# Expert results of an octet gathered in one transfer with 4 KB pieces, the last two octets from two queues, and stages separated by one meeting instead of two

## The reference

```python
x = x + tanh(g_xattn[0]) * L0_xattn(ctx, layernorm(x), mask, ...)   # 2 heads of 64, rms-normed q and k
x = x + tanh(g_ffn[0])   * L0_ffn(layernorm(x), ...)                # soft experts: 16 x 64 slots, hidden 256
x = x + tanh(g_xattn[1]) * L1_xattn(ctx, layernorm(x), ...)         # 8 heads of 128
x = x + tanh(g_ffn[1])   * L1_ffn(layernorm(x), ...)                # 8 experts, the best 2 of each token
```

```python
xf = x.reshape(N, D)                                   # N = 4096 tokens, D = 128
routing = softmax(xf @ router_w.T)                     # 8 experts
top_w, top_i = top_k(routing, 2); top_w = top_w / sum(top_w)
g = einsum('nd,ehd->neh', xf, w_gate); u = einsum('nd,ehd->neh', xf, w_up)
y = einsum('neh,edh->ned', silu(g) * u, w_down)        # hidden 256
out = einsum('ned,ne->nd', y, combine)                 # combine: top_w at the two experts, else 0
```

## Time and profile before

| what | us |
|---|---|
| three runs, median (lowest to highest) | 1481.29 (1478.18 to 1482.33) |
| span of the profiled execution | 1498.2 |
| PE busy in it | 1377.6 (92%) |
| ACT busy | 1012.3 (68%) |
| DVE busy | 953.4 (64%) |
| POOL busy | 523.2 (35%) |

### The profile page before, as it was taken

The page is one execution under the profiler, slowest core; times in us unless marked ns, Lnnn a source line. Parts: engine busy times, 40 slices in busy tenths (PEclk is TensorE's granted clock), DMA queues, the critical chain, the costliest instruction groups (busy, mean ns, idle before and its releaser), DMA issues. The chain is left out here.

```text
span 1498.2 us, 33716 instructions
## 1 busy us (share of the span) xinstructions
PE 1377.6 (92%) x12029; PEld 1171.5 (78%) x12029; DVE 953.4 (64%) x2374; ACT 1012.3 (68%) x2019; POOL 523.2 (35%) x510
## 2 busy tenths in 40 slices
PE   5898699899999999999999999988999999876985
PEld 4887588788888888888888888877778888755773
DVE  6998767666766767667667666552455555654455
ACT  5887487577677676776776767647788888633552
POOL 3112355322322322323223223302235555635553
PEclk9999899999999999999999999999999999998998
DMA  8300100399940000000000000022000000022236
GB/s 221 88 1 1 58 2 1 77 176 102 102 30 2 2 1 2 2 2 2 2 2 1 2 1 2 1 73 57 1 29 14 17 16 16 30 69 63 76 97 174
DMA packets 124980, 60.46 MB, mean 40 GB/s; under 512 B 41945, under 2 KB 120241, under 8 KB 124690
## 3 DMA queue, kind: packets, MB, share of 16 engines
q1 hardware_dynamic: 120274, 48.92, 18.2%
q0 software_dynamic: 4544, 9.38, 1.9%
HBM read 28.84 MB, written 29.44 MB: 39 GB/s over the span
## 5 line engine op out<-in xcount | busy, mean ns | idle before, releaser
L1349 DVE SCALAR_TENSOR_TENSOR hidden<-psU,b_cols,gelu 128x512 f32<-128x512 f32 x256 | 191.4, 750 | 170.1 <-ACT gelu L1474 104.9
L1474 ACT ACTIVATE gelu<-psG,b_cols 128x512 f32<-128x512 f32 x256 | 176.2, 689 | 109.6 <-PE psG L142 96.2
L1296 POOL TENSOR_TENSOR combine_sum<-combine_sum,combineT 128x512 f32<-128x512 f32 x48 | 63.3, 1319 | 294.9 <-ACT combineT L1488 294.9
L1325 POOL TENSOR_TENSOR dispatchT<-dispatchT,dispatch_inv 128x512 f32<-128x512 f32 x64 | 67.7, 1057 | 232.6 <-DVE dispatch_inv L1453 232.6
L1608 PE MATMUL psU<-w_down,hidden 128*64 128x128 f32 x2048 | 123.4, 273 | 0.0
L1608 PE MATMUL psDown<-w_down,hidden 128*64 128x128 f32 x2048 | 122.7, 273 | 0.0
L1861 POOL TENSOR_TENSOR probs<-probs,row_sum 128x512 f32<-128x512 f32 x64 | 66.2, 1035 | 143.6 <-DVE row_sum L1974 142.6
L1608 PEld LDWEIGHTS psU<-w_down,hidden 128*64 128x64 f32 x2048 | 113.2, 137 | 1.3 <-issue 1.2
L1608 PEld LDWEIGHTS psDown<-w_down,hidden 128*64 128x64 f32 x2048 | 113.9, 137 | 0.1
L140 PE MATMUL psG<-slots_hi,w_gate_hi 128*128 128x512 f32 x256 | 105.9, 414 | 1.1 <-ACT gelu L1474 0.6
L2038 ACT ACTIVATE probs<-psS,neg_max 128x128 f32<-128x128 f32 x256 | 91.2, 384 | 22.8 <-DVE neg_max L1971 18.4
(11 more groups left out here) (406 smaller groups left out, 3617.6 us busy)
## 6 DMA issues: line engine op xcount, KB each, us to landing
sorted_x<-empty_rows SPq DMA_DIRECT2D x1, 12736.0 KB, 77.5
tile_rows<-sorted_x SPq DMA_DIRECT2D x78, 65.0 KB
sorted_x<-empty_rows SPq DMA_DIRECT2D x1, 4544.0 KB, 29.9
expert_ys<-expert_y SPq DMA_DIRECT2D x16, 256.0 KB, 3.7
x<-in_x SPq DMA_DIRECT2D x8, 256.0 KB, 5.9
ctx<-in_ctx SPq DMA_DIRECT2D x8, 256.0 KB, 5.9
w_gate_raw<-in_L_ffn_Wg SPq DMA_DIRECT2D x1, 2048.0 KB, 10.9
w_up_raw<-in_L_ffn_Wu SPq DMA_DIRECT2D x1, 2048.0 KB, 16.1
```

What stands on the lines that cost most here:

```text
L1325: pool.tensor_tensor(e[:], e[:], over(rb[:], SEQ, 2), ALU.mult).then_inc(s["eb_normed"], 1)
L1349: dve.scalar_tensor_tensor(hid[e][:, half, :], U[half][:], bcol[:, 1, 4 * ch + 2 * e + half:][:, 0:1], gel[half][:], ALU.add, ALU.mult).th ...
L1474: act.activation(gel[half][:], G[half][:], ACT.Gelu, bias=bcol[:, 0, 4 * ch + 2 * e + half:][:, 0:1]).then_inc(s["gelu"], 1)
```

## The change

Four things are changed.

1. Home is now 8 p + 2 (t in the octet) + k, plus 1024 for each octet before it in the group. The eight results that partition p needs for one octet (four pairs, two choices) are eight rows in a row, 4096 bytes. `constants_vector` builds it with the same doubling steps; one instruction replaces the last two.
2. An octet is gathered in one transfer of 512 KB, 4096 bytes a partition, into `yin` with the choice behind the pair. Octets 0 to 6 are gathered by SP, octet 7 (`LAST`) by ACT, which waits for the same landed scatters at the end of its stream.
3. Of octet 7, DVE adds only the first two pairs (two adds of 128x256) and POOL the other two (two adds of 128x256, counted by the new semaphore `added_pool`); SP waits for both before its store.
4. `clear` no longer makes the engines meet, except after `stage_attention0` (`reused=True`). In exchange the semaphores of the stage just ended are kept out of the next one's choice.

```diff
-    def sem(self, ctx):
+    def sem(self, ctx, reused=False):
-        sems = []
+        sems, cleared = [], self.cleared
         def clear():
             self.nc.clear_and_free_semaphores(sems)
-            self.nc.all_engine_barrier()
+            if reused:
+                self.nc.all_engine_barrier()
+            self.cleared = [] if reused else [sem.num for sem in sems]
         def make(name):
-            sems.append(self.nc.alloc_semaphore(name=name))
+            num = [n for n in self.nc.free_semaphores if n not in cleared][0]
+            sems.append(self.nc.alloc_semaphore(name=name, num=num))
...
-        dve.tensor_copy(self.home[:, 0, 0:1], self.index[:]).then_inc(s["home"], 1)
-        for n, m in enumerate((1, 2, 4, 8, 16)):
+        dve.tensor_scalar(self.home[:, 0, 0:1], self.index[:], float(2 * OP), None, ALU.mult).then_inc(s["home"], 1)
+        for n, (m, step) in enumerate(((1, 2), (2, 4), (4, 2 * OT), (8, 4 * OT), (16, 8 * OT))):
...
-        for g, r in ((0, slice(0, first)), (1, slice(first, PAIRS))):
-            dve.tensor_scalar(self.home[:, 1, r], self.home[:, 0, r], float(self.groups[g].tokens), None, ALU.add
-                              ).then_inc(s["home"], 1)
+        dve.tensor_scalar(self.home[:, 1, :], self.home[:, 0, :], 1.0, None, ALU.add).then_inc(s["home"], 1)
...
+        def gather(eng, o):
+            group = R.groups[R.group_of(o)]
+            at = (o - group.octets[0]) * 2 * OT
+            eng.dma_start(yin[:, o, :, :, :].rearrange("p t k d -> p (t k d)"),
+                          group.ys[at:at + 2 * OT, :].rearrange("(p r) d -> p (r d)", p=P)).then_inc(y_loaded[o], 16)
...
-            for o in GROUPS[1]:
-                gather(o)
-            for o in GROUPS[1]:
-                store(o)
+            wait_stored(sp, len(QUADS) - 1)
+            gather(sp, LAST - 1)
+            store(LAST - 1)
+            sp.wait_ge(s["added"], 2 * OCTETS)
+            sp.wait_ge(s["added_pool"], 2)
+            sp.dma_start(tokens(c.out)[:, OP * LAST:OP * LAST + OP, :], c.x[:, OP * LAST:OP * LAST + OP, :]).then_inc(c.stored, 16)
...
+            pool.wait_ge(y_loaded[LAST], 16)
+            for k in range(2):
+                need(pool, s["added_pool"], k)
+                xo = c.x[:, OP * LAST + 2:OP * LAST + OP, :]
+                pool.tensor_tensor(xo, xo, yin[:, LAST, 2:OP, k, :], ALU.add).then_inc(s["added_pool"], 1)
...
-                xo = c.x[:, OP * o:OP * o + OP, :]
-                dve.tensor_tensor(xo, xo, yin[:, o, k, :, :], ALU.add).then_inc(s["added"], 1)
+                n = OP if o < LAST else 2
+                xo = c.x[:, OP * o:OP * o + n, :]
+                dve.tensor_tensor(xo, xo, yin[:, o, 0:n, k, :], ALU.add).then_inc(s["added"], 1)
...
+            wait_stored(act, len(QUADS) - 1)
+            gather(act, LAST)
```

More of the change, by code:

```diff
@@ L105, in __init__ @@
         self.stored = keep.enter_context(nc.semaphore("out_stored"))
+        self.cleared = []
     def sb(self, ctx):
@@ L239, in constants_vector @@
         first = self.groups[0].span
-        dve.tensor_copy(self.home[:, 0, 0:1], self.index[:]).then_inc(s["home"], 1)
-        for n, m in enumerate((1, 2, 4, 8, 16)):
+        dve.tensor_scalar(self.home[:, 0, 0:1], self.index[:], float(2 * OP), None, ALU.mult).then_inc(s["home"], 1)
+        for n, (m, step) in enumerate(((1, 2), (2, 4), (4, 2 * OT), (8, 4 * OT), (16, 8 * OT))):
             dve.wait_ge(s["home"], n + 1)
             w = min(m, first - m)
-            dve.tensor_scalar(self.home[:, 0, m:m + w], self.home[:, 0, 0:w], float(m * P), None, ALU.add
+            dve.tensor_scalar(self.home[:, 0, m:m + w], self.home[:, 0, 0:w], float(step), None, ALU.add
                               ).then_inc(s["home"], 1)
@@ L612, in stage_attention0 @@
     with ExitStack() as ctx:
-        sb, sem = c.sb(ctx), c.sem(ctx)
+        sb, sem = c.sb(ctx), c.sem(ctx, reused=True)
         ready = Ready(c, lined_up(nc))
@@ L2249, in stage_experts1 @@
         to = [sb(f"tile_to{i}", [P, OP], U32) for i in range(SPARE)]
-        yin = sb("expert_ys", [P, OCTETS, 2, OP, D])
+        yin = sb("expert_ys", [P, OCTETS, OP, 2, D])
         XT, ROUTE = c.bank(ctx, "psXT"), c.bank(ctx, "psRoute")
@@ L2255, in stage_experts1 @@
         Y = [c.bank(ctx, f"psY3_{i}") for i in range(2)]
-        names = "xt x_hi x_lo gu silu hidden ht ht_copied down scaled to_ready added"
+        names = "xt x_hi x_lo gu silu hidden ht ht_copied down scaled to_ready added added_pool"
         s = {n: sem("d_" + n) for n in names.split()}
@@ L2262, in stage_experts1, with wait_stored @@
         block = ctx.enter_context(nc.Block())
+        def gather(eng, o):
[3 more added lines that the diff above has]
+                          group.ys[at:at + 2 * OT, :].rearrange("(p r) d -> p (r d)", p=P)).then_inc(y_loaded[o], 16)
+        def wait_stored(eng, q):
+            for last in range(q + 1 - SPARE, q + 1):
+                eng.wait_ge(stored[last % SPARE], 16 * upto(last, SPARE))
         @block.sync
@@ L2269, in load @@
                 R.load_tiles(sp, q)
-            def gather(o):
-                group = R.groups[R.group_of(o)]
-                at = (o - group.octets[0]) * OT
-                for k in range(2):
-                    sp.dma_start(yin[:, o, k, :, :], group.ys[k * group.tokens + at:k * group.tokens + at + OT, :]
-                                 .rearrange("(t p) d -> p t d", p=P)).then_inc(y_loaded[o], 16)
             def store(o):
-                need(sp, s["added"], 2 * (o + 1))
+                sp.wait_ge(s["added"], 2 * (o + 1))
                 sp.dma_start(tokens(c.out)[:, OP * o:OP * o + OP, :], c.x[:, OP * o:OP * o + OP, :]).then_inc(c.stored, 16)
@@ L2285, in _ @@
                 load(q)
-            for last in range(QUAD[NA - 1] + 1 - SPARE, QUAD[NA - 1] + 1):
-                sp.wait_ge(stored[last % SPARE], 16 * upto(last, SPARE))
+            wait_stored(sp, QUAD[NA - 1])
             for o in GROUPS[0]:
-                gather(o)
+                gather(sp, o)
             for o in GROUPS[0]:
                 store(o)
-            for last in range(len(QUADS) - SPARE, len(QUADS)):
-                sp.wait_ge(stored[last % SPARE], 16 * upto(last, SPARE))
-            for o in GROUPS[1]:
-                gather(o)
-            for o in GROUPS[1]:
-                store(o)
+            wait_stored(sp, len(QUADS) - 1)
[4 more added lines that the diff above has]
+            sp.dma_start(tokens(c.out)[:, OP * LAST:OP * LAST + OP, :], c.x[:, OP * LAST:OP * LAST + OP, :]).then_inc(c.stored, 16)
             sp.wait_ge(c.stored, 16 * OCTETS)
@@ L2349, in add @@
             def add(o, k):
-                dve.wait_ge(y_loaded[o], 32)
+                dve.wait_ge(y_loaded[o], 16)
                 need(dve, s["added"], 2 * o + k)
-                xo = c.x[:, OP * o:OP * o + OP, :]
-                dve.tensor_tensor(xo, xo, yin[:, o, k, :, :], ALU.add).then_inc(s["added"], 1)
+                n = OP if o < LAST else 2
+                xo = c.x[:, OP * o:OP * o + n, :]
+                dve.tensor_tensor(xo, xo, yin[:, o, 0:n, k, :], ALU.add).then_inc(s["added"], 1)
             x_lo(0)
```

## The result

The changed kernel takes 1484.70 us (median of 9 executions, 1482.79 to 1487.88), the kernel before 1481.35 us (9 executions, 1478.18 to 1482.33). The ratio is 1.0029, with a 95% interval of 1.0019 to 1.0039, which is 4.3 us (2.8 to 5.8). The forecast was 1479.6 us, a range of 1476.2 to 1482.0 and a chance of 0.10 for slower.

The account below looks back on a forecast made before the run. PE was busy 92%, but gains were sought where every engine waits: the stage borders and the end's chain of waits. Terms -0.7 - 0.7 - 0.5 + 0.2 = -1.7 us took 1481.29 to 1479.6 us, range 1476.2 to 1482.0.

Parts of the forecast that it names:

- added waits: At the end, SP's wait for POOL's adds has only the last store behind it; no cost was counted.
- dear scatters: Rival: the new row spacing makes POOL's last-stage scatters take 1.85 us each, 9 us more, 1488.6 us; chance 0.08.
- closing drains: At the end, POOL's two drains of 0.10 us and its clears remain, so dropping two meetings wins 0.5 us.
- Second meetings: Four meetings go: 0.7 us won at each of two inner borders and 0.5 us at the end.
- Gathers: Octets 6 and 7 land together at 1490.9, after 1.4 us fixed and 2.6 us of transfer at 406 GB/s.
- Larger pieces: Rival: 4096-byte pieces in the last gathers still move at 280 GB/s, sum -0.5 us, 1480.8 us; chance 0.18.
- The fixed part: Start cost of a last gather, taken as 1.4 us from the last store's 2.3 us wait.
- Adds in turns: DVE's and POOL's last adds wait for each other, taking 3.6 us and ending at 1494.5, a term of +0.2 us.
- Ending 7.4 to 7.8 us after SP's first gather: Sign that the forecast is right: the last adds end then, against 7.35 us before.
- octet 6's store: Near the end, this store was expected to have gone out 1 us sooner than before.
- Hidden edits: Gathers of octets 0 to 5, constants and row spacing count 0; bounds for the last scatter's landing -0.2 to +1.8 us.

Follow-up runs that it names:

- share_only: The kernel before with only POOL's two adds of octet 7 added: 1483.82 us against 1479.24 us, ratio 1.0035.
- no_share: The changed kernel with all last adds on DVE and none on POOL: 1477.85 us against 1479.24 us for the kernel before, ratio 0.9995.
- early_drain: The changed kernel with one more drain of POOL ahead of its two adds: 1478.59 us against 1479.24 us for the kernel before, ratio 1.0001.
- meetings_only: The kernel before without the second meetings except after the first stage: 1478.37 us against 1479.24 us, ratio 0.9991.
- one_queue: The changed kernel with all adds on DVE and both last gathers issued by SP: 1477.06 us against 1478.31 us for the kernel before, ratio 0.9988.
- the second comparison: The changed kernel measured again, unchanged, against the kernel before: 1484.07 us against 1478.42 us, ratio 1.0033.

## Why the prediction was wrong, point by point

**The step that failed** is in the part on added waits: "SP waits for POOL's adds with only the last store behind". It looked at what stands behind the waiting SP and not at what stands behind POOL's adds. There stood the block's closing drain, a row of the very line that I quoted for SP's branch, and it was 8.95 us long. Moved behind the adds, it ended at 1485.19 where SP was ready at 1480.8. This is worth 4.6 us by SP's wait and 5.3 us in the end of share_only (4.6 by its medians), and it disappears in no_share and early_drain. None of the rivals had it; the one that ended slower, dear scatters, was tested and is not so.

I had also counted the closing drains as two of 0.10 us, from the line that clears semaphores. That was right for those two. The Trainium skill (VectorE: DVE Perf Modes, The DRAIN you can't avoid) gives "~12 ns constant" for the drains that the runtime puts at the start and end of a kernel on all five engines. These here carry the line of the program's own block, SP's is 7 ns and POOL's 8849 ns long, so that figure is not to be carried over to them.

**Second meetings, a second step that failed.** "At the two inner borders each engine starts 0.7 us sooner" held, but the sum took it for 1.4 us of the total. The third stage took 321.1 to 321.3 us from release to release in seven of eight profiles without the second meeting, against 320.6 to 320.8 in three of four with it, since the granted clock fell to 0.50 for 3.4 us in the former (meetings_only). So the traces give the two inner borders about nothing, +0.5 and -0.2 us. At the end the gain was 0.6 us in meetings_only (0.5 forecast), and the last meeting lies 0.74 us before the end of the span (0.7 forecast, 1485.36 to 1486.1).

**Gathers: both landed 4.0 us after the issue.** Measured 4.70. That they would come together was right (they landed 4.68 and 4.88 us after SP's issue). The rate was near, as the windows of the changed kernel show, which answer to the earlier trace rows (stretch, us, five busy times, PEclk, DMA share, GB/s):

```profile
1471.30:1472.00 0.70, 0.00 (x0) 0.00 (x0) 0.00 (x0) 0.00 (x0) 0.00 (x0) 0.50 1.27 94
1472.00:1474.50 2.50, 0.00 (x0) 0.00 (x0) 0.00 (x0) 0.00 (x0) 0.00 (x0) 0.50 0.92 377
```

Over 2.5 us it is 377 GB/s, the fading end included, against 280 GB/s for rows of 512 bytes. Larger pieces do gain. The 512 B that the Trainium skill gives for line rate (DMA: Bandwidth & Descriptors, Specifications) is not where the gain ends here. Mis-sized was the start: 94 GB/s until 1472.0. In this profile the first sixteen pieces of 4096 bytes took 0.67 to 1.08 us (median 0.92), and 236 of the 240 others 159 ns. Slow first pieces are not the reason, though: in no_share, with the same two gathers, the first sixteen took 0.16 to 0.76 us and the last piece was over only 0.07 us sooner (4.39 against 4.46 us after the issue). What sets the start stays open. The fixed part, 1.4 us from a store by one queue, was 2.1 us here (4.7 less the 2.6 us of 1 MB at 406 GB/s). What this does to the adds one_queue shows: from one queue octet 6 is in use after 3.49 us. Two transfers that share the engines both end late, and the adds need the first one early.

**Adds in turns.** Seen, but weaker than put down. In the chain above DVE's adds beside POOL's take 1.04 instead of 0.70 us (128x512) and 0.77 instead of 0.42 (128x256). Each of POOL's two adds costs DVE 0.35 us, not the 0.65 of a full turn, so 3.21 us from first to last instead of 3.6. "Ending 7.4 to 7.8 us after SP's first gather" became 7.91: 0.7 later by the landing, 0.4 sooner by the adds, a term of +0.5 to +0.6 in place of +0.2. Nor did octet 6's store go out sooner than before: 6.55 us after the first gather, against 5.34. What the step did not ask is what four adds on DVE alone take: 3.08 us. The sharing won nothing before its drain was counted.

**Hidden edits.** The gathers of octets 0 to 5, the constants and the spacing of scattered rows cost nothing that shows: POOL's scatters stay 1.27 us apart, and no_share is at 0.9995 of before.

**The sum with what was measured:** about 0 (inner borders, from the traces) -0.6 (end meetings) +0.5 (landing and adds) +4.6 (drain) = +4.5 us. The ends in the table give the same, 15.79 against 11.28. Measured are 3.35 by the medians and 2.8 to 5.8 by the ratio; the second comparison gives 5.65 and 3.0 to 6.7. Without the drain the sum is near 0 and not near the forecast of -1.7: no_share's end is 0.2 us shorter than that of before, and its time -0.7 us (-2.1 to +0.6), which does not tell it from nothing.

The chance of 0.10 for slower covered little beyond the one mechanism that I had named. The instruction that counted stands on no chain and in no list of costs.

## What to carry to other kernels

Before an engine gets the last piece of work, read what already stands behind its present last one, the block's closing drain too: here a drain of POOL after 94 indirect transfers took 7.75 us and needed cover. If POOL must work at the end, drain it once where it waits anyway, and not close behind scatters that are still landing. Where a chain begins with the first of two transfers, try both from one queue in the order of use; here a second queue only made the first one late. And read a gain at a stage's start again at its end: here 0.7 us won at a border were mostly gone within 30 us.

## What the runs showed of the hardware that I had not expected

- POOL's drain took about 0.083 us for each indirect transfer since the last drain: 1.54 us for 18, 4.02 for 48, 6.28 for 76, 7.75 for 94. Directly behind four scatters it ended 0.20 us after the last of them had landed, 1.46 us after its end at the least. Its record names no releaser, and it is not counted as busy.
- From two queues the first octet was in use after 4.62 to 4.91 us, from one after 3.47 to 3.49, for the same bytes on the same engines.
- The first sixteen pieces of 4096 bytes behind a pause took 0.67 to 1.08 us in the changed kernel and 0.16 to 0.76 us in no_share, most of the following ones 159 ns.
- The granted clock fell to 0.50 for 3.4 us about 12 us into the third stage in six of eight profiles that started it 0.7 us sooner, and took the gain back; in three of four with the second meeting it did not.
- A wait at a meeting was put down to PE, which had been done for 14 us when SP came to it; the last one was POOL.
